# Self-attention rewritten in a decoder layer of float32: paired projections, values as the stationary operand, the maximum subtracted on GpSimd, operands placed at multiples of 1 KB

## The reference

```python
def self_attention(h, Wq, Wkv, Wo):       # 32 heads of 16, one key and value head for all
    q = (h @ Wq).reshape(b, s, 32, 16)
    k, v = split(h @ Wkv)                 # 16 and 16 wide
    scores = einsum('bqhd,bkd->bhqk', q, k) * 16 ** -0.5 + slopes * (pos_k - pos_q)   # causal
    return einsum('bhqk,bkd->bqhd', softmax(scores), v).reshape(b, s, 512) @ Wo

x = x + self_attention(layernorm(x), ...)
x = x + cross_attention(layernorm(x), ctx, ctx, positions, mask, ...)   # 32 heads of 128, 8 kv heads, rotary
x = x + feed_forward(layernorm(x), ...)                                # 1376 wide, silu(gate) * up
```

## Time and profile before

| | |
|---|---|
| median of 3 runs | 1015.9 us |
| the profiled execution | 1015.93 us, its span 1014.1 us |
| PE busy | 987.1 us, 97% |
| PEld, DVE, ACT, POOL busy | 809.2, 589.1, 429.5, 382.2 us |
| granted clock of PE, mean | 0.992 |

### The profile page before, as it was taken

One profiled execution on the slowest core, in us unless ns is written; L12 is line 12 of the kernel. 1 busy time (PEld: TensorE's weight loads), 2 busy tenths in 40 slices (PEclk: granted clock), 3 DMA queues, 4 the chain that ended last, 5 costly groups with the idle time before them and its releaser, 6 DMA issues. The chain is left out here.

```text
span 1014.1 us, 15751 instructions
## 1 busy us (share of the span) xinstructions
PE 987.1 (97%) x5128; PEld 809.2 (80%) x5128; DVE 589.1 (58%) x973; ACT 429.5 (42%) x1239; POOL 382.2 (38%) x375
## 2 busy tenths in 40 slices
PE   5999999989999999999999999999999989999998
PEld 3877777877888888888888888888888768888787
DVE  3755566645776676666666767657666773343100
ACT  2776776761433533523533533533432543333100
POOL 7422222163562642652642643634623422222200
PEclk8999999989999999999999999999999999999999
DMA  6000000211120210210210210210200112222001
GB/s 202 13 11 11 11 10 10 63 52 52 32 63 11 54 52 0 70 33 0 72 31 0 72 31 0 73 31 11 83 1 0 33 32 66 69 68 70 10 32 42
DMA packets 49954, 39.98 MB, mean 39 GB/s; under 512 B 4128, under 2 KB 40096, under 8 KB 49920
## 3 DMA queue, kind: packets, MB, share of 16 engines
q1 hardware_dynamic: 49536, 38.48, 12.8%
q0 software_dynamic: 384, 1.05, 0.3%
HBM read 37.43 MB, written 2.10 MB: 39 GB/s over the span
## 5 line engine op out<-in xcount | busy, mean ns | idle before, releaser
L624 PE MATMUL bank<-cross_wo_hl,cross_outT_hl 128*128 128x512 f32 x768 | 191.7, 398 | 1.0 <-POOL cross_wo_hl L618 0.6
L624 PE MATMUL bank<-hsT_hl,cross_wqkv_hl 128*128 128x512 f32 x768 | 188.2, 394 | 0.0
L624 PEld LDWEIGHTS bank<-cross_wo_hl,cross_outT_hl 128*128 128x128 f32 x768 | 143.1, 188 | 35.6 <-POOL cross_wo_hl L618 1.6
L624 PEld LDWEIGHTS bank<-hsT_hl,cross_wqkv_hl 128*128 128x128 f32 x768 | 141.9, 188 | 29.3
L938 ACT ACTIVATE cross_scores<-cross_scores,cross_negmax 128x128 f32<-128x128 f32 x256 | 99.8, 391 | 127.1 <-DVE cross_negmax L876 127.1
L798 POOL TENSOR_TENSOR cross_qT<-rotated,rotated_other_half 128x512 f32<-128x512 f32 x64 | 82.8, 1293 | 161.8 <-DVE rotated_other_half L840 161.8
L624 PE MATMUL bank<-hsT_hl,ff_gate_upT_hl 128*128 128x512 f32 (+1 forms) x528 | 120.4, 390 | 2.7 <-DVE ff_gate_upT_hl L1140 2.7
L624 PEld LDWEIGHTS bank<-hsT_hl,ff_gate_upT_hl 128*128 128x128 f32 (+1 forms) x528 | 97.7, 185 | 25.0 <-DVE ff_gate_upT_hl L1140 3.1
L948 ACT CAST cross_outT_hl<-bank 128x512 fp32r<-128x512 f32 x64 | 37.1, 580 | 143.3 <-PE bank L624 142.4
L838 DVE TENSOR_TENSOR rotated<-bank,cosT 128x512 f32<-128x512 f32 x80 | 55.2, 690 | 71.2 <-PE bank L624 71.1
L624 PE MATMUL bank<-ctxT_hl,cross_wqkv_hl 128*128 128x512 f32 x384 | 94.2, 394 | 1.1 <-PEq L74 1.1
(11 more groups left out here) (117 smaller groups left out, 1539.7 us busy)
## 6 DMA issues: line engine op xcount, KB each, us to landing
staged_rows<-in_wq SPq DMA_DIRECT2D x32, 256.0 KB, 2.8
staged_rows<-in_wo SPq DMA_DIRECT2D x32, 256.0 KB, 2.7
staged_rows<-in_wg SPq DMA_DIRECT2D x10, 256.0 KB, 2.9
staged_rows<-in_wu SPq DMA_DIRECT2D x10, 256.0 KB, 2.9
staged_rows<-in_wd SPq DMA_DIRECT2D x10, 256.0 KB, 2.9
ctx_tok<-in_ctx SPq DMA_DIRECT2D x8, 256.0 KB, 2.6
staged_rows<-in_wk SPq DMA_DIRECT2D x8, 256.0 KB, 3.0
staged_rows<-in_wv SPq DMA_DIRECT2D x8, 256.0 KB, 3.1
```

The costliest lines, as they stand in the source:

```text
L624: i = nc.tensor.matmul(out, stationary[:, a], moving[:, b], start=(first and k == 0), stop=(last and k == 2))
```

## The change

**Projections for pairs.** xn of a pair of sequences (b even and odd) is transposed into hsT, split in halves, and q is projected already transposed, with a tile of Wq stationary and the 256 columns of the pair moving, in two portions u (in steps 1 and 4 of odd sequences). q's transposes and the copies of q_hl go. Keys and values of a pair come in step 4 of even sequences. Wq, Wk and Wv are split at the start, in memory that later holds ctx. The output is a product of halves too, so attnT is split: ACT's `attn_high`, DVE's `attn_low`.

**Values stationary.** v with 16 columns of ones (32 columns) is loaded as the weights, in four column tiles of the array, and the transposed probabilities move. The result comes transposed, is copied by ACT (`copy_out`) and transposed back on PE (`out_back`) before DVE normalises it.

**The maximum.** POOL adds the negated maximum (`below_max`, L194), ACT does one exponential of 512 columns in place. S and negmax are rings of four steps.

**Loads.** ctx comes transposed from memory, two sequences at a time; the pieces of cross-attention's first weights come in another order (`FIRST_PIECES`); the rotation tables are gathered to cosT and sinT after POOL's last subtraction. DVE makes 12 of the 32 biases.

**Borders.** Small tensors are laid out first or last and a pad of 128 bytes stands before the large ones.

```diff
+PAD = 32
+RING = 4
+BIAS_DVE = 12
@@ GpSimd
-            for h in range(HEADS):
+            def below_max(n):
+                pool.wait_ge(sem["max1"], n + 1)
+                nc.gpsimd.tensor_tensor(S[:, n % RING], S[:, n % RING], negmax[:, n % RING, :].unsqueeze(2).to_broadcast([P, QUAD, P]), ALU.add).then_inc(sem["shifted1"], 1)
+            for h in range(BIAS_DVE, HEADS):
                 nc.gpsimd.tensor_scalar(bias[:, h, :], rel[:], slopes[h], None, ALU.mult).then_inc(sem["bias"], 1)
-                if h == 15:
+                if h == 16:
                     pool.wait_ge(sem["head_of_row_loaded"], 16)
                     keys_by_head(0)
+            for b in range(SEQS):
+                for s in range(STEPS):
+                    below_max(STEPS * b + s)
+                    if b == 0 and s == 0:
+                        rstd_of_x(2, SEQS, 3)
+                    if s == 0 and b < SEQS - 1:
+                        keys_by_head(b + 1)
+                    if s == 2 and 2 <= b:
+                        hs_of(b - 2)
...
@@ VectorE
+            def q_low(p, u, bank):
+                dve.wait_ge(sem["q_high"], 2 * p + u + 1)
+                for r in range(2):
+                    own = qT[:, p % 2, bass.ds(4 * u + r, 2, 2), :]
+                    e = nc.vector.tensor_tensor(own[64:128], bank[64 * r:64 * r + 64, :].rearrange("p (i k) -> p i k", i=2), own[0:64].bitcast(F32), ALU.subtract)
+                e.then_inc(sem["q_low"], 1)
...
+                    if b == 0 and s == 0:
+                        q_low(0, 1, G[0])
+                        dve.wait_ge(sem["x_rest"], 16)
+                        for c in (2, 3, 4):
+                            stats_of_x(c)
+                    if b == 0 and s == 1:
+                        for c in (5, 6, 7):
+                            stats_of_x(c)
...
+                    if s == 6 and b >= 1:
+                        attn_low(b - 1)
@@ ScalarE
-                        for j in range(QUAD):
-                            e = nc.scalar.activation(PR[:, s % 2, j, :], S[:, s % 2, j, :], ACT.Exp, bias=negmax[:, s % 2, j:j + 1])
-                        e.then_inc(sem["exp1"], 1)
+                        act.wait_ge(sem["shifted1"], n + 1)
+                        nc.scalar.activation(S[:, n % RING], S[:, n % RING], ACT.Exp).then_inc(sem["exp1"], 1)
@@ TensorE
+            def kv_product(p):
+                pe.wait_ge(sem["xnT_low"], 2 * p + 2)
+                for t in range(KT):
+                    products(nc, G[0][:, 0:2 * P], wk8[:, :, t], block_of(hsT[:, :, t], p, 2 * P), t == 0, t == KT - 1)
...
+            def q_product(p, u, bank):
+                for i in range(2):
+                    at = (2 * u + i) * P
+                    for t in range(KT):
+                        e = products(nc, bank[:, 2 * P * i:2 * P * (i + 1)], wq[:, :, t, at:at + P], block_of(hsT[:, :, t], p, 2 * P), t == 0, t == KT - 1)
+                e.then_inc(sem["q1"], 1)
...
+            def out_back(b, i):
+                pe.wait_ge(sem["out_copied"], 2 * b + i + 1)
+                for s in range(HALF):
+                    e = nc.tensor.transpose(OB[i][:, s * P:(s + 1) * P], oc[:, s, :], ident[:])
+                e.then_inc(sem["out_back"], 1)
...
-                            i = nc.tensor.matmul(OB[r // HALF][:, c:c + HD1 + 1], PT[:, r % 2, j, :], v[:, bass.ds(owner, 1), :].rearrange("p b d -> p (b d)"),
+                            i = nc.tensor.matmul(OB[r // HALF][32 * j:32 * j + 32, (r % HALF) * P:(r % HALF + 1) * P], v[:, owner, :], PT[:, r % 2, j, :],
                                                  start=True, stop=True)
...
@@ memory
+        sb("up_to_a_multiple_of_1_KB", [P, PAD])
+        stage = sb("staged_rows", [P, SLOTS, DM])
```

More of the change, by code:

```diff
@@ L372, in body @@
+            xnT_high(0, G[0])
+            xnT_high(1, G[1])
+            act.wait_ge(sem["wq1_loaded"], 32)
+            for u in range(2):
+                for h in range(2):
+                    nc.scalar.copy(wq[:, 0, 2 * h:2 * h + 2, 2 * u * P:2 * (u + 1) * P], wq_rows[h][:, :, 2 * u * P:2 * (u + 1) * P]).then_inc(sem["wq1_high"], 1)
+                if u == 0:
+                    k_high(0)
+            q_high(0, 0, G[1])
+            q_high(0, 1, G[0])
             def body(b):
-                scores, front = not since(b, SEQS), not since(b, SEQS - 1)
@@ L422, in _ @@
-            for b in range(3):
-                body(b)
-            with act.Fori(3, SEQS - 1) as b:
-                body(b)
-            for b in range(SEQS - 1, SEQS + 1):
+                    if b == 0 and s == 1:
+                        act.wait_ge(sem["wo1_loaded"], 16)
+                        nc.scalar.copy(wo[:, 0], wo_rows).then_inc(sem["wo1_high"], 1)
+                    if s == 7 and scores:
+                        copy_out(b, 0)
+                    if s == 3 and b >= 1:
+                        copy_out(b - 1, 1)
@@ L427, in _ @@
+            for b in range(SEQS + 1):
                 body(b)
@@ L482, in body @@
+            pe.wait_ge(sem["wq1_low"], 2)
+            q_product(0, 0, G[1])
+            pe.wait_ge(sem["wq1_low"], 4)
+            pe.wait_ge(sem["kv_copied"], 1)
+            q_product(0, 1, G[0])
             def body(b):
-                scores, front = not since(b, SEQS), not since(b, SEQS - 1)
-                back = since(b, 1)
+                scores = b < SEQS
                 for s in range(STEPS):
```

636 lines of the change are left out of this document (326 added, 310 removed).

## The result

The changed kernel takes 1059.6 us (median of 4 runs, 1057.1 to 1063.5) against 1015.9: ratio 1.043, 95% interval 1.040 to 1.046. The direction was forecast, the size was not: +19 us forecast, +43.7 measured, 1.6 us above the upper end of the range.

The account below looks back on a forecast made before the run. The prediction took the kernel to be a queue of TensorE matmuls nearly everywhere. From 1014.1 us, start +19, sequences +14, tail +4 and borders -18 gave 1033, with 1.8 outside the span 1035 us; range 1000 to 1058.

Parts of the forecast that it names:

- Start, +19: Up to the second sequence: GpSimd's queue waits on VectorE's statistics, second sequence at 60 instead of 41.2 us; +12 to +24.
- TensorE's own work: Self-attention sequences: TensorE's products and transposes alone fall from 25.3 to 22.3 us a sequence.
- 0.65 a step: Values product on four column tiles: records overlap only in part, 0.65 us a step, between 0.22 and 0.87.
- the 0.87 a step: Values product if column tiles run one after the other: 0.87 us a step, seven sequences some 198 us.
- Waits in a sequence, +14: Seven middle sequences: waits take back what TensorE saves, 190 us in all against 175.9.
- (b): Seventh step, output: TensorE waits for attnT_low, 3.5 us in odd sequences, 2.3 in even, about 2 in the last two.
- (a): Third step: hs stands behind GpSimd's subtraction, so TensorE waits 2.1 to 3.0 us in each of six sequences.
- rival 2: Seven sequences: TensorE's waits pull its clock down, 17 us more, 1052 us; chance 0.13.
- Tail, +4: After the last sequence: rotation-table gathers stand behind GpSimd's last subtraction, 22 us against 18.0 to the first cross product.
- Borders, -18: Products after self-attention: operands at multiples of 1 KB save 6.7 us plus ~4 ns in each of 2904 products.
- Rival 1: Whole kernel: GpSimd's answers hidden and borders giving 18 to 41 us, 985 to 1008 us; chance 0.23.
- rival 4: Self-attention: the four-step ring hides the subtraction, sequences save 20 us, borders give 0 to 7; 1012 to 1022; chance 0.08.

Follow-up runs that it names:

- e3: Changed kernel with another order in the start alone (statistics before the first maximum, 24 biases on VectorE, keys and xn before GpSimd's first subtraction): 1041.8 us.
- e6: Changed kernel with 126 needless 512-column products added at the places where TensorE waits: 1046.4 us.
- e7: Changed kernel with one call moved: VectorE's attn_low ahead of kv_low and q_low: 1037.3 us.
- e11: Changed kernel with only the eight rotation-table gathers moved from behind GpSimd's last subtraction into the first, third and fifth sequence: 1051.6 us.
- e12: e10 plus fills of 2 to 7 needless products at places where TensorE still waits: 995.2 us.
- e1: Kernel before the change with the borders alone (pad, small tensors last, large operands at multiples of 1 KB): 1010.5 us, ratio 0.995.
- e9: Changed kernel with e3's start, e7's order, copy_out and hs earlier in odd b and the last two sequences, and e11's gathers: 1005.8 us.
- e10: e9 with ScalarE subtracting the maximum again, by four exponentials with a bias, in place of GpSimd: 998.8 us.

## Why the prediction was right and wrong

- **Start, +19 against +21.7: right, and by its reason.** GpSimd waits on VectorE's statistics from 32.6 to 39.9 (30 to 37 forecast), TensorE for xn. e3 takes the cause away and 17.7 us with it. Some 3 of the 21.7 us are chance: where the faster pace came earlier (first scores at 26.4 to 26.8 in e6, e7 and e11) the second sequence starts at 59.9 to 60.3. Not foreseen: 4.1 us in which TensorE waits for the second half of q's weights, split behind q_low(0, 0) on VectorE (PE L698 <- DVE ctxT_hl L284).
- **TensorE's own work: too high.** At 22.3 us a sequence seven take 156; the estimate from e12 is 141. Part of the 15 is that the 22.3 gives every sequence its projections, and the last two have none. The values, put at 0.65 a step, measure 0.36. My 0.65 let only two records in turn overlap and added something for the change of tile shape. No run shows either as a rule: in the trace four run at once, and 0.36 a step is what they take. The transposes ahead of them take 0.10 more than before: the values' first record starts 0.203 us behind the last transpose, where 0.109 is the pace, and the next full-width product 0.202 behind the values' last record. The tiles change from 128\*128 to 128\*32 and back at these two places; whether that is the cause no kernel tests. The overlap is real: tiles one behind the other, the 0.87 a step that the range had room for, are out.
- **Waits in a sequence, +14 against +23.7: what failed is half rate, put at nothing.** The waits themselves were priced well. (b), the wait for attnT_low, is 4.0 us in odd sequences (3.5 forecast), 2.3 in even ones (2.3) and 1.4 in the last two (2), 19.5 in all. (a), the third step's wait of 2.1 to 3.0 in six sequences, measures 1.9 to 2.8, but half of its cause was missed: TensorE stands first for the copy of the output on ScalarE (14.8 us in eight, 2.8 the longest) and then, in four of the six, 0.2 to 0.7 for hs (2.2 in all). I had gone through the queues of GpSimd and VectorE and not through ScalarE's. Then came half rate: I had made it rival 2, +17 us in place of my forecast, while e6 shows it as a companion of the waits, 13.2 us. Waits as in the forecast and a clock that holds did not go together here: from the second sequence to the first cross product the granted clock was 0.87 with the waits and 0.98 in e6.
- **That the sequences miss by only 10 is partly luck.** Over the seven, TensorE is idle 41.3 us (199.6 less 158.3), where 190 less 156 leaves 34; its products take 158.3 us instead of 141, so 17 us more by the slower clock, where the forecast had none. So 15 us too much of own work hid more than half of the 24 that waits and clock were short (an estimate: the 190 were laid out step by step, and only their sums are on record). Sequence by sequence (b = 1 to 7) the forecast was 27, 27, 29.6, 27, 29.6, 25, 24.5, measured are 31.7, 27.4, 31.5, 27.4, 32.4, 24.9, 24.2: the miss lies in b = 1, 3 and 5, which have 10.2, 6.8 and 10.2 us of half rate, against 3.4 in b = 2 and 4 and 6.8 in b = 6.
- **Tail, +4 against +3.2: right.** e11 shows that all of it is the place of the gathers. The "1.2 GHz" of the working stands for the granted clock of 0.50, which the trace shows from 220.5 to 230.7 us; no row gives a frequency.
- **Borders, -18 against -5 (e1; -3.1 in the profiled run, with the stretch of half rate, some 3 us): the largest miss, mis-sized by 13 to 15 us.** Shown were 7 ns in 960 products, 6.7 us. The other 11 us rested on the estimate that an aligned product takes 0.215, from a pair of weight loads 0.43 apart; 780 aligned products say 0.227. A product at 896 bytes had nothing to heal. The working has a slip too: half of 12 ns is 6 and not 4, and by this sum would have given 24 us. Rival 1 needed this gain, and rival 4 waits that never show; both are out.
- The sum misses by 26.7 us of span (1059.7 against 1033): borders 15, sequences 10, start 3, tail -1. Some 6 of these come from stretches at half rate that not every profile of the same code has, 3 in the start and 3 in the rest. Two slips of the working change nothing: the figures of (a) give 2.1 to 2.6, not 3.0, and those of rival 4 end at 1019, not 1022.

Not settled: how GpSimd's 7 us in e9 against e10 divide between the longer chain and its busier queue; how the 0.10 us before the values arise; and what the new projections give without the new values, since no kernel had one alone.

## What to carry over

When work goes from a full engine to others, write down every in-order queue that the full one then depends on, and look for the call that stands behind one that waits for later work: here one call moved on VectorE was worth some 20 us, nearly half of the loss. Where two engines' results are waited for in one place, as the output's copy and hs are here, mending one shows only the other. Waits on TensorE are priced with the half rate that follows them (58.0 us of it here, 13.2 us of time by e6), not as an alternative to it. And a saving that only an estimate supports is kept at what a row shows until a run says more.
